# Second attention: ranks ahead of values, divisions on ACT, and two reciprocal roots on DVE

## The chip, the cores and the metric

The kernel runs on one core of a Trainium2 chip. The metric is the device time of one execution in microseconds. TensorE is called PE here, VectorE DVE, ScalarE ACT, GpSimd POOL and SyncE SP.

## The reference

A network of six residual stages over x of 2048 rows (4 batches of 512) and 128 features: a routed feed-forward, a landmark attention, the feed-forward again, a feed-forward with 32 experts (top 4) and a shared part, a windowed attention, and the experts once more. The change lies in the last two, cut to this:

```python
x = x + _L1_attn_ref(_layernorm(x), ...)      # B, S = 4, 512
    q, k, v = x @ Wq + bq, x @ Wk + bk, x @ Wv + bv
    scores = einsum('bwqd,bwkd->bwqk', qw, kw) / sqrt(8)   # 7 windows of 128 at steps of 64
    out_w = einsum('bwqk,bwkd->bwqd', softmax(scores), vw) # summed over windows, / counts
    return out @ Wo + bo
x = x + 0.5 * _L1_ffn_ref(_layernorm(x), ...)
    topk_scores, topk_idx = top_k(softmax(flat @ router_w.T + router_bias), 4)
    # 32 experts: silu(gate) * up, down; sum of the 4 chosen ones by normalised score
    out = out + silu(flat @ sgate_w.T) * (flat @ sup_w.T) @ sdown_w.T    # shared part
```

## The kernel before

The program is written engine by engine: each engine runs its instructions in the order written, and waits on counting semaphores. Rows are handled in four groups of 512, which are also the batches of this attention.

`attn1` is the second attention. For batch b, PE projects q, k and v (`project_q`, L2446, and so on), computes seven score windows (`scores`, L2469) into two banks, the even windows (half 0) in one and the odd (half 1) in the other. DVE takes the maxima (`maximum`, L2351), ACT the exponentials with their sums (`exp`, L2288), DVE the reciprocals and the products (`scale`, L2358 and L2359), PE the transposes of the weights (`turned`, L2476), ACT copies them (`evict`, L2296), PE multiplies by the values (`values`, L2485), ACT averages (`averages`, L2304), PE projects out (`output`, L2499), and DVE adds to x (`residual`, L2364).

The routing of the last stage is woven in one batch behind. For group g = b - 1: statistics on DVE ("variance", L200 to L205), the power -0.5 on POOL (`power`, L211), the normalisation on DVE ("normalised", L218), transposes on PE (L227), their copy on ACT (`copy`, L232), router logits on PE (L539), and on DVE the pieces "scores" (L482), "top", "hot", "counted", "weights" and "rows". "rows" begins with L519, which needs the ranks that PE computes in `tensor_rank` (L548 to L554, waiting for the mask of "counted"), and ends with L521, which gives the row numbers. POOL then sends the group's rows to `sorted_rows` in 16 indirect DMAs (`pool_dispatch`, L469): dispatch g. POOL's powers stand at written places between these issues: those of the attention's own groups 2 and 3 too (`norm`; `srt.norm` is the routing's).

Group 3's routing runs in the eight shared-expert steps behind the attention (L416 to L418 are their gate and up matmuls, L710 the silu, L717 the product, L749 the down matmuls); the table LATE says at which step each piece stands. Step 0 to 2 also make the first table of tiles (L660 is its last part). Then the quad loop begins: 20 quads of four pairs of 64-row tiles, each with transposes of the loaded tile (L1024), their copy on DVE (L939), the expert's matmuls and four indirect DMAs on POOL for the results. Quads 0 to 3 need dispatches 0 and 1, quads 4 to 7 dispatch 2, those from 8 dispatch 3.

At the start of the attention the last two groups of the stage before are still being summed: POOL adds pairs of returned rows (`pool_pair`), DVE adds the rest (`vector_combine`), in pieces spread over batches 0 and 1, and POOL's powers for `norm` follow.

Of the kernel before, what the change touches and what calls it, by code (L numbers as in the profile page):

```python
# [10 lines left out]
I32 = mybir.dt.int32  # L11
ALU = mybir.AluOpType
ACT = mybir.ActivationFunctionType
AX = mybir.AxisListType.X
P = 128
# [17 lines left out]
def build(nc, a, out):  # L33
# [8 lines left out]
    with ExitStack() as ctx:  # L42
# [30 lines left out]
        mv = sb("mv", [P, NT, 2])  # L73
        rstd = sb("rstd", [P, NT])
# [114 lines left out]
        class Norm:  # L189
# [3 lines left out]
            def __init__(self, first, order=None):  # L193
                self.first, self.order = first, order or range(first, first + NG)

            def statistics(self, g, ready):
# [8 lines left out]
                DVE.tensor_scalar(rstd[:, 4 * g:4 * g + 4], mv[:, 4 * g:4 * g + 4, 1], 1e-5, None, ALU.add).then_inc(*var_ready.inc)  # L205
# [7 lines left out]
            def normalise(self, g):  # L213
                DVE.wait_ge(*rstd_ready(self.order[g] + 1))
# [6 lines left out]
            def transposes(self, g, meanwhile=0, b=6):  # L221
                if self.order[g]:
                    PE.wait_ge(*xT_ready(self.order[g]))
                keep_busy(meanwhile, bank[6])
                PE.wait_ge(*xn_ready(self.order[g] + 1))
# [8 lines left out]
            def transposed(self, g):  # L234
                return xT_transposed(self.order[g] + 1)

            def ready(self, g):
                return xT_ready(self.order[g] + 1)


        norms = [Norm(NG * n) for n in range(4)] + [Norm(16, (16, 17, 19, 21)), Norm(20, (18, 20, 22, 23))]
# [178 lines left out]
        class Sorted:  # L420
# [40 lines left out]
            def pool_dispatch(self, g, power_after, other_after=(), other_norm=None):  # L461

                POOL.wait_ge(*rows_ready(g + 1))
                for i in range(4 * TOPK):
                    if i == power_after and g < NG - 1:
                        self.norm.power(g + 1)
                    if i in other_after:
                        other_norm.power(2 + other_after.index(i))
# [285 lines left out]
            def tiles(self, room):  # L754
# [353 lines left out]
                for s in (mask_ready, rank_mm, rows_ready, shared_added, combined, sorted_low_ready):  # L1108
                    s.ends(NG)
                pair_added.ends(2)  # L1110
# [41 lines left out]
            def vector_combine(self, g):  # L1152
# [4 lines left out]
                yield  # L1157
                DV(DVE.tensor_tensor(xg, b[:, :, 1, :], xg, ALU.add))
                yield
                DVE.wait_ge(*self.paired[g])  # L1160
                DVE.tensor_tensor(xg, self.pair[g], xg, ALU.add).then_inc(*combined.inc)
                yield
# [29 lines left out]
        def ffn0(updated, outer, norm, srt=None, following=None):  # L1192
# [58 lines left out]
            def pool_engine():  # L1251
# [29 lines left out]
                if srt:  # L1281
                    POOL.wait_ge(*zeroed(NE))
                    for g, transfers in enumerate((6, 4, 3, 0)):
                        srt.pool_dispatch(g, transfers)
# [940 lines left out]
        def attn1(earlier, outer, norm, srt):  # L2225
# [18 lines left out]
            sc_mm, mw_ready, ew_ready, ew_scaled = (signal(n) for n in ("sc_mm", "mw_ready", "ew_ready", "ew_scaled"))  # L2244
# [21 lines left out]
            def scalar_engine():  # L2266
# [46 lines left out]
                for b in range(B):  # L2313
                    if b:
                        srt.norm.copy(b - 1)
# [316 lines left out]
```

## Time and profile before

| what | value |
|---|---|
| median of 3 runs | 977.83 us (975.63 to 982.14) |
| the profiled execution's own time | 978.78 us |
| its span, first to last instruction | 977.3 us |
| granted clock of TensorE, mean share | 0.896 |
| busy: PE, DVE, ACT, POOL | 763.2, 548.9, 400.1, 443.1 us |

The span leaves 1.5 us of the execution outside it. Busy time is a sum of instructions; what it leaves of the span is waiting, and in this kernel no engine is near full, so the table alone names no bound.

### The profile page before, as it was taken

The page shows a single profiled execution, that of the slowest core. Times are in us where ns is not written, and L with a number is a line of the kernel's source. Part 1 is how long each engine was busy: PE and PEld are TensorE (multiplying, and loading weights), DVE is VectorE, ACT ScalarE, POOL GpSimd, SP SyncE. Part 2 cuts the span into 40 slices and gives each one's busy share as a digit, 9 for nine tenths or more (in the row PEclk, how much of TensorE's full clock was granted, in tenths as well). Part 3 has the DMA queues.
Part 4 walks back from the last instruction along what each step waited for, and adds up shares of the span by engine and source line. Part 5 has one row for each costly group of instructions (what it writes and reads, how often), then busy time and mean ns, then how long its engine had stood idle before and what let it go on. Part 6 is the DMA issues. An engine that isn't in the chain of part 4 may idle for free.

```text
span 977.3 us, 19551 instructions
## 1 busy us (share of the span) xinstructions
PE 763.2 (78%) x6738; PEld 578.4 (59%) x6738; DVE 548.9 (56%) x1656; ACT 400.1 (41%) x967; POOL 443.1 (45%) x484
## 2 busy tenths in 40 slices
PE   7979989899998898867377766788788537667767
PEld 6868756699765786755254444466566424444446
DVE  6974776578655985755345233365865415333345
ACT  4647554654363554531133334326332213333421
POOL 4646602446002546445625545541666444544551
PEclk9999998999999999888688778899888859877889
DMA  9999994900543501001233222402111222232253
GB/s 230 213 220 219 221 218 92 190 4 4 114 77 129 196 1 45 27 33 50 71 78 80 73 74 69 140 28 87 36 46 44 61 54 67 66 72 75 75 170 97
DMA packets 121056, 93.99 MB, mean 96 GB/s; under 512 B 14208, under 2 KB 111872, under 8 KB 120576
## 3 DMA queue, kind: packets, MB, share of 16 engines
q1 hardware_dynamic: 104288, 70.00, 31.9%
q0 software_dynamic: 9216, 19.68, 6.0%
q10 hardware_dynamic: 7456, 3.07, 1.5%
q8 instruction: 55, 0.90, 0.4%
q14 instruction: 41, 0.34, 0.1%
HBM read 31.76 MB, written 57.41 MB: 91 GB/s over the span
## 4 chain that ended last, share of the span: by engine, by line
PE 40%; DVE 21%; another core or an unknown queue 16%; issue 9%; ACT 8%; POOL 3%; ACTq 2%; DMA 1%; DVEq 0%; POOLq 0%
PE banks L2064 5%; PE banks L1047 4%; PE banks L749 3%; PE banks L1054 2%; PE banks L1442 2%; POOL sorted_rows L469 2%; ACT routed_scratch L875 2%; DVE hT L1351 2%; PE banks L416 2%; PE banks L418 2%; PE banks L417 2%; DVE rows_x L218 2%; PE banks L1062 2%; ACTq L912 1%
## 5 line engine op out<-in xcount | busy, mean ns | idle before, releaser
L854 POOL DMA_INDIRECT expert_rows<-y,goal x160 | 155.4, 971 | 165.9 <-DVE goal L950 87.5
L469 POOL DMA_INDIRECT sorted_rows<-rows_x,row_of x128 | 127.2, 994 | 105.5 <-DVE row_of L521 69.8
L1047 PE MATMUL banks<-routed_w,t 128*64 x320 | 104.3, 484 | 43.1 <-DVE t L939 42.7
L1310 ACT ACTIVATE ys<-banks,wtab 128x128 f32<-128x128 f32 x256 | 73.1, 370 | 81.5 <-PE banks L1442 62.0
L1047 PE MATMUL banks<-routed_scratch,t 128*64 128x256 f32 x320 | 104.9, 485 | 0.3 <-issue 0.2
L956 DVE TENSOR_TENSOR h<-sg,banks 128x512 f32<-128x512 f32 x40 | 27.5, 687 | 131.5 <-ACT sg L884 103.8
L1047 PEld LDWEIGHTS banks<-routed_w,t 128*64 128x64 f32 x320 | 51.6, 173 | 81.1 <-issue 71.0
L416 PE MATMUL banks<-x_high,w_high 128*128 128x512 f32 x192 | 87.4, 455 | 0.8 <-POOL w_low L1189 0.4
L1442 PE MATMUL banks<-w,hT 128*128 128x128 f32 x512 | 71.9, 284 | 19.2 <-DVE hT L1351 18.5
L1442 PEld LDWEIGHTS banks<-w,hT 128*128 128x128 f32 x512 | 65.7, 196 | 28.6 <-issue 22.2
L418 PE MATMUL banks<-x_high,w_low 128*128 128x512 f32 x192 | 78.8, 410 | 3.1 <-issue 3.1
L417 PE MATMUL banks<-x_low,w_high 128*128 128x512 f32 x192 | 78.6, 409 | 1.1 <-issue 1.1
L1236 POOL TENSOR_TENSOR x<-ys,x 128x512 f32<-128x512 f32 x43 | 55.0, 1279 | 52.5 <-ACT ys L1310 52.2
L892 ACT COPY hT<-banks 128x512 f32<-128x512 f32 x40 | 23.4, 585 | 120.3 <-remote 58.5
L875 ACT COPY routed_scratch<-routed_w 128x384 f32 x160 | 69.8, 510 | 5.5 <-issue 5.5
L211 POOL TENSOR_TENSOR rstd<-rstd,mhalf 128x4 f32<-128x4 f32 x24 | 26.4, 1101 | 99.0 <-DVE rstd L205 98.9
L1062 PE MATMUL banks<-routed_w,hT 128*64 x320 | 50.9, 305 | 25.0 <-issue 13.0
L884 ACT ACTIVATE sg<-banks 128x512 f32<-128x512 f32 x40 | 23.8, 594 | 97.1 <-PE banks L1047 52.1
L1351 DVE TENSOR_TENSOR hT<-sg,banks 128x512 f32<-128x512 f32 x64 | 43.8, 684 | 29.4 <-ACT sg L1318 23.5
L1062 PEld LDWEIGHTS banks<-routed_w,hT 128*64 128x64 f32 x320 | 39.3, 152 | 31.1 <-issue 30.9
L1054 PE MATMUL banks<-ident,h 128*128 128x128 f32 x160 | 31.4, 328 | 32.2 <-DVE h L956 23.7
L1062 PE MATMUL banks<-routed_scratch,hT 128*64 128x128 f32 x320 | 51.3, 306 | 6.0 <-issue 6.0
(362 smaller groups left out, 1787.9 us busy)
## 6 DMA issues: line engine op xcount, KB each, us to landing
sorted_rows<-zeros SPq DMA_DIRECT2D x32, 1120.0 KB, 16.8
tile<-sorted_rows SPq DMA_DIRECT2D x252, 35.0 KB
routed_w<-in_ffn_w SPq DMA_DIRECT2D x8, 768.0 KB, 11.7
w<-in_ffn_w SPq DMA_DIRECT2D x20, 192.0 KB, 5.3
expert_rows<-y,goal POOLq DMA_INDIRECT x160
tile<-sorted_rows ACTq DMA_DIRECT2D x68, 35.0 KB
qS<-x_high SPq DMA_DIRECT2D x8, 256.0 KB, 6.0
sorted_rows<-rows_x,row_of POOLq DMA_INDIRECT x128
```

The lines of the kernel that those rows point to most:

```text
L416: PE.matmul(ps, expert.high[:, n, :], x_high[:, cols], start=True, stop=False)
L417: PE.matmul(ps, expert.high[:, n, :], x_low[:, cols], start=False, stop=False)
L418: return PE.matmul(ps, expert.low[:, n, :], x_high[:, cols], start=False, stop=True)
L469: POOL.indirect_dma_start(sorted_rows, bass.IndirectOffsetOnAxis(self.row_of[:, g, i:i + 1], 0), rows_x[:, 4 * g + i // TOPK, :], None).th ...
L854: POOL.indirect_dma_start(expert_rows, bass.IndirectOffsetOnAxis(goal[:, 4 * q + i:4 * q + i + 1], 0), y[q % 6][:, i * P:(i + 1) * P], Non ...
L875: last = SCL.copy(odd[q % 3][:, i, :], routed.w[:, bass.ds(expert[4 * q + i], 1), :].rearrange("p o c -> p (o c)"))
L1047: last = PE.matmul(pairs(q)[ROWS * h:ROWS * h + ROWS, i, :], t[q % 2][:, rows], weights(q, i, h, slice(0, 2 * P)), start=True, stop=True)
L1062: last = PE.matmul(bank[7][ROWS * h:ROWS * h + ROWS, i * P:(i + 1) * P], hT[q % 2][:, rows], weights(q, i, h, slice(2 * P, 3 * P)), start= ...
L1236: engine.tensor_tensor(xg, ys[s % 2][:, :].rearrange("p (j d) -> p j d", d=D), xg, ALU.add).then_inc(*added.inc)
L1310: last = SCL.mul(ys[s % 2][:, j * P:(j + 1) * P], bank[4 + s % 2][:, j * P:(j + 1) * P], wtab[:, t, e:e + 1])
L1351: DVE.tensor_tensor(hT[s % 2][:, :], sg[s % 2][:, :], bank[2 + s % 2][:, :], ALU.mult).then_inc(*hidden_done.inc)
L1442: last = PE.matmul(bank[4 + s % 2][:, j * P:(j + 1) * P], hT[s % 2][:, j * P:(j + 1) * P], experts[s % rows].w[:, 2, :], start=True, stop= ...
```

## The change

In the attention's batches 1 to 3, DVE makes only the reciprocals (`reciprocals`), and ACT multiplies the windows (`divide`). The order on all engines is written anew: PE computes the ranks of a group ahead of the batch's values, ACT copies the routing's transposes behind both exponentials in batches 2 and 3, the two sums of the stage before stand together ahead of batch 0's residual, and some projections and their evictions move forward. POOL makes both powers of `norm` ahead of dispatch 0, and that of routing group 1 after its fourth issue. The routing norms of groups 2 and 3 get their reciprocal root on DVE (`root`: a shift and a multiply-add on the bits, then three Newton steps), so POOL makes no power within dispatches 1 and 2. LATE moves each piece of group 3 one step later. Signals of `Norm` get an order for the transposes (`turn`) apart from that of the powers.

```diff
     class Norm:
-            def __init__(self, first, order=None):
+            def __init__(self, first, order=None, turn=None, rooted=()):
...
-                DVE.tensor_scalar(rstd[:, 4 * g:4 * g + 4], mv[:, 4 * g:4 * g + 4, 1], 1e-5, None, ALU.add).then_inc(*var_ready.inc)
+                variance = DVE.tensor_scalar(rstd[:, 4 * g:4 * g + 4], mv[:, 4 * g:4 * g + 4, 1], 1e-5, None, ALU.add)
+                if g in self.rooted:
+                    DV(variance)
+                    self.root(g)
+                else:
+                    variance.then_inc(*var_ready.inc)
+
+            def root(self, g):
+                v, y = rstd[:, 4 * g:4 * g + 4], guess[:, :]
+                DVE.tensor_scalar(half_var[:, :], v, -0.5, None, ALU.mult)
+                DV(DVE.tensor_scalar(y.bitcast(I32), v.bitcast(I32), 1, None, ALU.arith_shift_right))
+                DV(DVE.tensor_scalar(y.bitcast(I32), y.bitcast(I32), -1.0, float(0x5f3759df), ALU.mult, ALU.add))
+                for n in range(3):
+                    DV(DVE.tensor_tensor(square[:, :], y, y, ALU.mult))
+                    DV(DVE.tensor_tensor(square[:, :], square[:, :], half_var[:, :], ALU.mult))
+                    DV(DVE.scalar_tensor_tensor(out=y if n < 2 else v, in0=square[:, :], scalar=1.5, in1=y, op0=ALU.add, op1=ALU.mult))
...
             def normalise(self, g):
-                DVE.wait_ge(*rstd_ready(self.order[g] + 1))
+                if g not in self.rooted:
+                    DVE.wait_ge(*rstd_ready(self.order[g] + 1))
...
-        norms = [Norm(NG * n) for n in range(4)] + [Norm(16, (16, 17, 19, 21)), Norm(20, (18, 20, 22, 23))]
+        norms = [Norm(NG * n) for n in range(4)] + [Norm(16, (16, 17, 19, 20), (16, 17, 19, 21)), Norm(20, (18, 21, 22, 23), (18, 20, 22, 23), (2, 3))]
...
-            LATE = dict(normalised=1, transposes=2, copy=2, logits=3, split=3, scores=3, top=4, hot=4, counted=4, exp=4, rank=5,
-                        weights=5, rows=5, low=6)
+            LATE = dict(normalised=2, transposes=3, copy=3, logits=4, split=4, scores=4, top=5, hot=5, counted=5, exp=5, rank=6,
+                        weights=6, rows=6, low=7)
...
@@ pool_engine @@
                 srt.norm.power(0)
-                srt.pool_dispatch(0, 8, (3, 9), norm)
-                srt.pool_dispatch(1, 3)
-                srt.pool_dispatch(2, 1)
-                srt.pool_dispatch(3, 0)
+                POOL.wait_ge(*xn_ready(srt.norm.turn[0] + 1))
+                norm.power(2)
+                norm.power(3)
+                srt.pool_dispatch(0, {4: 1})
+                srt.pool_dispatch(1, {})
+                srt.pool_dispatch(2, {})
+                srt.pool_dispatch(3, {})
...
@@ scalar_engine @@
+                def divide(b, h):
+                    SCL.wait_ge(*sums_ready(2 * b + h - 1))
+                    for k in range(len(HALVES[h])):
+                        w = WA * h + k
+                        last = SCL.mul(Ew[h][:, k, :], Ew[h][:, k, :], sw[:, b, w:w + 1])
+                    last.then_inc(*ew_divided.inc)
...
-                for b in range(B):
-                    if b:
-                        srt.norm.copy(b - 1)
...
+                srt.norm.copy(0)
+                exp(1, 0)
+                exp(1, 1)
+                srt.scalar_exp(0)
+                divide(1, 0)
+                divide(1, 1)
...
+                for b in (2, 3):
                     exp(b, 0)
                     exp(b, 1)
+                    srt.norm.copy(b - 1)
+                    divide(b, 0)
+                    divide(b, 1)
+                    srt.scalar_exp(b - 1)
+                    if b == 2:
+                        norm.copy(3)
                     evict(b, 0)
+                    if b == 2:
+                        evict_q(3)
                     evict(b, 1)
+                    if b == 2:
+                        evict_k(3)
                     averages(b)
+                    srt.scalar_split(b - 1)
+                    if b == 2:
+                        evict_v(3)
...
@@ vector_engine @@
+                def reciprocals(b, h):
+                    total = sw[:, b, WA * h:WA * h + len(HALVES[h])]
+                    DVE.wait_ge(*ew_ready(2 * b + h + 1))
+                    DVE.reciprocal(total, total).then_inc(*sums_ready.inc)
...
+                earlier.vector_combine(2)
+                earlier.vector_combine(3)
+                residual(0)
+                routed_piece(0, "variance")
+                norm.statistics(2, earlier.combined[2])
+                routed_piece(0, "normalised")
+                maximum(1, 0)
+                maximum(1, 1)
+                norm.statistics(3, earlier.combined[3])
+                routed_piece(0, "scores")
+                reciprocals(1, 0)
+                routed_piece(0, "top")
+                reciprocals(1, 1)
+                for piece in ("hot", "counted", "weights", "rows"):
+                    routed_piece(0, piece)
+                norm.normalise(2)
+                residual(1)
+                routed_piece(1, "variance")
+                for b in (2, 3):
+                    if b == 3:
+                        maximum(3, 0)
+                        maximum(3, 1)
+                    routed_piece(b - 1, "normalised")
+                    srt.vector_low(b - 2)
+                    if b == 2:
+                        maximum(2, 0)
+                        maximum(2, 1)
+                        norm.normalise(3)
+                    reciprocals(b, 0)
+                    reciprocals(b, 1)
+                    for piece in ("scores", "top", "hot", "counted", "weights", "rows"):
+                        routed_piece(b - 1, piece)
                     residual(b)
                     routed_piece(b, "variance")
...
@@ tensor_engine @@
+                for b in range(1, B):
                     scores(b, 0)
                     scores(b, 1)
+                    srt.norm.transposes(b - 1)
+                    if b > 1:
                         keep_busy(2, bank[5 - b % 2])
+                    srt.tensor_logits(b - 1)
+                    if b == 1:
+                        keep_busy(2, bank[4])
+                    if b == 2:
+                        norm.transposes(3)
+                    turned(b, 0)
                     if b == 1:
                         srt.tensor_rank(0)
                         PE.wait_ge(*earlier.shared[3])
-                    turned(b, 0)
                     turned(b, 1)
-                    values(b, 0)
-                    values(b, 1)
+                    if b == 2:
+                        project_q(3)
                     if b > 1:
                         srt.tensor_rank(b - 1)
+                    values(b, 0)
+                    if b == 2:
+                        project_k(3)
+                    values(b, 1)
+                    output(b)
                     if b == 1:
-                        output(1)
                         norm.transposes(2, 0, 7)
                         project_q(2)
...
```

## Rows read from the trace of the kernel before

**Rows 1.** The chain of waits that ended last, its share of the span by engine.

```profile
PE 40%; DVE 21%; another core or an unknown queue 16%; issue 9%; ACT 8%; POOL 3%; ACTq 2%; DMA 1%; DVEq 0%; POOLq 0%
```

**Rows 2.** Busy time by stretch (start:end, length, each engine's busy us and instructions).

```profile
740.00:779.00 39.00, 30.55 (x164) 23.92 (x162) 24.01 (x91) 9.04 (x19) 19.75 (x20) 0.86 0.18 51
779.00:794.00 15.00, 0.00 (x1) 0.00 (x0) 1.95 (x4) 0.23 (x1) 11.34 (x13) 0.58 0.26 72
```

**Rows 3.** POOL in order of time: start, us, instruction, idle time before and its end.

```profile
688.21 1.44 POOL L469 DMA_INDIRECT sorted_rows<-rows_x,row_of  x1 [10.57 <-DVE row_of L521]
...
711.79 0.95 POOL L469 DMA_INDIRECT sorted_rows<-rows_x,row_of  x1 [0.30 <-issue]
715.98 0.95 POOL L469 DMA_INDIRECT sorted_rows<-rows_x,row_of  x1 [3.24 <-DVE row_of L521]
...
719.88 1.04 POOL L211 TENSOR_TENSOR rstd<-rstd,mhalf 128x4 f32<-128x4 f32 x1
...
736.76 0.95 POOL L469 DMA_INDIRECT sorted_rows<-rows_x,row_of  x1 [0.30 <-issue]
741.50 0.95 POOL L469 DMA_INDIRECT sorted_rows<-rows_x,row_of  x1 [3.78 <-DVE row_of L521]
...
762.98 0.95 POOL L469 DMA_INDIRECT sorted_rows<-rows_x,row_of  x1 [0.30 <-issue]
775.62 0.95 POOL L469 DMA_INDIRECT sorted_rows<-rows_x,row_of  x1 [11.69 <-DVE row_of L521]
...
794.59 0.95 POOL L469 DMA_INDIRECT sorted_rows<-rows_x,row_of  x1 [0.30 <-issue]
```

**Rows 4.** DVE in order of time, 700 to 794 us.

```profile
701.21 1.28 DVE L218 TENSOR_SCALAR rows_x<-x,mv,rstd 128x128 f32<-128x128 f32 x4 [1.86 <-POOL rstd L211]
...
714.09 0.69 DVE L519 TENSOR_TENSOR r_home<-r_home,banks 128x512 f32<-128x512 f32 x1 [2.21 <-remote]
...
720.96 1.28 DVE L218 TENSOR_SCALAR rows_x<-x,mv,rstd 128x128 f32<-128x128 f32 x4 [1.94 <-POOL rstd L211]
...
739.61 0.69 DVE L519 TENSOR_TENSOR r_home<-r_home,banks 128x512 f32<-128x512 f32 x1 [7.27 <-remote]
...
756.38 0.28 DVE L660 CAST table<-banks 1x128 int32<-1x128 f32 x1 [3.27 <-remote]
...
766.86 0.49 DVE L482 MAX8 top<-banks 128x8 f32<-128x32 f32 x4 [9.06 <-remote]
...
793.30 0.69 DVE L939 COPY t<-banks 128x512 f32<-128x512 f32 x1 [6.34 <-remote]
```

**Rows 5.** PE in order of time, 688 to 779 us.

```profile
688.88 1.73 PE L2476 MATMUL banks<-ident,Ew 128*128 128x128 f32 x7 [3.31 <-DVE Ew L2359]
...
732.18 0.75 PE L554 MATMUL banks<-r_home,ones 128*128 128x96 f32 x6
...
737.77 2.07 PE L2499 MATMUL banks<-Wo,oT 128*128 128x128 f32 x8 [3.90 <-issue]
739.50 0.77 PE L416 MATMUL banks<-x_high,w_high 128*128 128x512 f32 x1
...
755.88 0.98 PE L539 MATMUL banks<-Wr,xnT 128*128 128x32 f32 x8
...
778.40 0.60 PE L1024 MATMUL banks<-ident,tile 128*128 128x128 f32 x4
```

**Rows 6.** Prices: order of time on DVE and ACT, and DVE's groups, 663 to 740.

```profile
711.16 0.29 DVE L513 TENSOR_SCALAR red_a<-red_a 128x4 f32<-128x4 f32 x1
...
373.15 1.14 ACT L1310 ACTIVATE ys<-banks,wtab 128x128 f32<-128x128 f32 x4 [0.69 <-issue]
...
703.30 0.58 ACT L232 COPY xnT<-banks 128x512 f32<-128x512 f32 x1 [1.76 <-PE banks L227]
...
706.19 0.25 ACT L459 ACTIVATE power<-power 128x16 f32<-128x16 f32 x1
...
L2359 DVE TENSOR_TENSOR Ew<-Ew,sw 128x512 f32<-128x512 f32 (+1 forms) x8 | 5.6, 705 | 0.3
```

More of the change, by code:

```diff
@@ L1107, in tiles @@
                 tensor_engine()
-                for s in (mask_ready, rank_mm, rows_ready, shared_added, combined, sorted_low_ready):
+                for s in (mask_ready, rank_mm, rows_ready, shared_added, sorted_low_ready):
                     s.ends(NG)
+                combined.ends(NG)
                 pair_added.ends(2)
@@ new lines, in scalar_engine @@
+                exp(0, 1)
+                evict_v(0, (1,))
+                evict(0, 0)
+                evict(0, 1)
+                norm.copy(1)
+                averages(0)
+                SCL.wait_ge(*earlier.back_here[2])
+                evict_q(1)
+                evict_k(1)
+                evict_v(1)
+                srt.norm.copy(0)
[4 more added lines that the diff above has]
+                divide(1, 1)
+                evict(1, 0)
@@ L2384, in vector_engine @@
                 last_shared_add()
-                for b in range(B):
-                    if b:
-                        maximum(b, 0)
-                        maximum(b, 1)
-                        if b == 1:
-                            next(third)
-                        elif b == 2:
-                            norm.normalise(3)
-                        for piece in ("scores", "top"):
-                            routed_piece(b - 1, piece)
-                        if b > 1:
-                            scale(b, 0)
-                            scale(b, 1)
-                        for piece in ("hot", "counted", "weights", "rows"):
-                            routed_piece(b - 1, piece)
-                        if b == 1:
-                            scale(b, 0)
-                            scale(b, 1)
-                            next(third)
-                            norm.statistics(2, earlier.combined[2])
-                            for _ in fourth:
-                                pass
-                            norm.normalise(2)
+                earlier.vector_combine(2)
@@ L2408, in vector_engine @@
                     residual(b)
                     routed_piece(b, "variance")
-                    if b == 0:
-                        next(third)
-                    elif b == 1:
-                        norm.statistics(3, earlier.combined[3])
-                    if b > 1:
-                        srt.vector_low(b - 1)
-                    if b < LAST:
-                        routed_piece(b, "normalised")
-                    if b == 1:
-                        srt.vector_low(0)
+                srt.vector_low(2)
```

92 lines of the change are left out of this document (39 added, 53 removed).

## The prediction

> **What bounds the kernel now.** I first read the chain that ended last [rows 1]: PE leads with 40% of the span, DVE has 21%, and 16% is "another core or an unknown queue", which on one core can only be a wait whose end came without a releaser that the trace knows. So no engine bounds the kernel; a relay of waits does. The stretch that the change touches is the second attention with its routing (about 663 to 740 us), the eight shared-expert steps behind it (740 to 779) and the start of the quad loop. The table by stretch [rows 2] shows PE busy 30.55 of 39 us in the shared steps, and then not at all from 779 to 794.
>
> POOL's own order comes next [rows 3]. Its four dispatches of 16 indirect DMAs each begin at 688.21, 715.98, 741.50 and 775.62. An issue every 1.265 us follows from the last one (775.62 to 794.59, 15 steps), so 16 take 20.2 us. POOL waited 3.24, 3.78 and 11.69 us ahead of dispatches 1, 2 and 3, each time for the row numbers (L521).
>
> DVE's and PE's rows say why the row numbers were late [rows 4, 5]. Rank matmuls of group 2 (L554) end at 732.18 + 0.75 = 732.93, but DVE's L519, which waits for them alone, starts at 739.61: 6.7 us of "remote". The logits of group 3 (L539) end at 756.86 and their reader starts at 766.86: 10 us. The transposes of the first tile (L1024) end at 779.00 and their copy (L939) starts at 793.30: 14.3 us. At 714.09 it is 2.21 us, at 756.38 3.27. All lie in the later part of a dispatch or just behind it: 711.79, 736.76 and 762.98 are the last issues of dispatches 0, 1, 2, and the signal came 2.3, 2.9 and 3.9 us behind them [rows 3, 4]; the copy of the first tile came 1.3 us ahead of the last issue of dispatch 3. I call this a hold: PE's signal waits while POOL dispatches. I have no cause for it, only its places. What is on the path is therefore POOL's stream with the holds at its ends.
>
> **Batch 1: divisions leave DVE.** Before, DVE scaled the weights behind all of group 0's routing, and PE waited 3.31 us for it, to 688.88 [rows 5]. Now only two reciprocals stand between the routing pieces, and ACT multiplies window by window. Four ACT multiplies of 128x128 by a column took 1.14 us [rows 6], so seven take 2.0 us, on an engine that had nothing to do then. The wait of 3.3 us goes, and the rank matmuls now stand between the two halves, which gives or takes 1 us: values, output and the projections of batch 2 come 3 to 5 us earlier. The reciprocals and the two statistics pushed ahead delay group 0's row numbers, dispatch 0 with them, by 0.5 to 1 us. The two other norms' powers now precede it; they are ready by then, so they cost no path.
>
> **Dispatch 0.** It took from 688.21 to 711.79 + 1.26 = 713.05 with three powers inside: 24.8 us. With one, 16 issues and one power of about 1.5 make 21.8. From 689.1 it ends at 711, 2 us earlier, with its power after 4 issues and not after 8, thus 4 x 1.265 = 5 us earlier. DVE's wait of 1.86 us at 701.21 [rows 4] goes with that.
>
> **Batch 2.** ACT's copy of the routing's transposes now stands behind both exponentials: before, the copy began at 703.30 and the exponentials ran to 706.19 [rows 6], about 2.4 us, which the logits now wait for. Against it stand the 5 us of the power, and two DVE scalings of 0.705 us [rows 6] that no longer lie between "top" and "hot". Sum for the row numbers of group 1: 2.4 - 5 - 1.4 = -4.0, to which the held 2.2 us may be added. They were there at 715.7, and are now at 709.5 to 714.5; so dispatch 1 starts between the end of dispatch 0, 711, and 714.5 (before 715.98), the later value if a hold still meets the ranks.
>
> **Batch 3: the root on DVE.** The power of group 2 sat in POOL's queue behind three issues of dispatch 1 (719.88), and DVE stood 1.94 us ahead of 720.96 [rows 3, 4]. Instead DVE runs 12 small dependent instructions. Their like (L513, 128x4) took 0.29 us at most [rows 6], and 0.2 with the shorter ones around it; I take 12 x 0.21 = 2.5 us, between 2.0 and 3.5. The trace shows no shift of bits; I price it as the other small ones. The Trainium skill, VectorE: DVE Perf Modes, section on the TRN2 errata, gives some 150 cycles of fixed cost to an instruction; by that the root would be an estimated 12 x 0.156 = 1.9 us, 0.6 less than my sum. Two maxima now also precede the normalisation, about 1.2 us by L2359's 0.705 for the same widths, while a subtraction of some 0.6 moves behind it. So seen from the residual this piece gains nothing (2.5 + 1.2 against 1.94 + 0.6, about +1); scalings off DVE give 1.4 back, the rest of batch 3 is what batches 1 and 2 hand on.
>
> **Ranks ahead of values.** The ranks of groups 1 and 2 no longer queue behind 14 value matmuls, some 2 us by the 0.60 that four transposes of that width took [rows 5]. Group 2's would end near 732.9 - 4 - 2 = 727, ahead of where their hold was. Then dispatch 2 waits only for dispatch 1: 711 to 714.5 + 20.2, so 731 to 735, middle 733, against 741.50: -8.5. The end of the attention (first shared matmul, 739.50 [rows 5]) held, at 737.77, a wait of 3.9 us behind held signals. I leave a hold of that size in, since values still lie late in dispatch 1, and take 732 to 736.
>
> **The combined sums, LATE and the end.** Two residual sums and their statistics move to a DVE that idled there: nothing, unless back rows are late. LATE puts every piece of group 3 one step later; a step is about 2.3 us ((756.86 - 739.50 - 3.27) / 6). Group 3's power leaves POOL (1.3 us of dispatch 2) and costs 2.5 us on DVE, under the first step. Dispatch 2 from 733 has its last issue 19 us later, 752; as before the hold ends 3.9 us behind, 755.9. The logits of group 3, now at step 4, are made near 734 + 13 + 2.3 = 749, inside it. From release to dispatch 3 were 8.8 us (766.86 to 775.62 [rows 3, 4]); so dispatch 3 starts at 764.7, or 767 if the later step shows in full: -9 to -11. If dispatch 2 starts at 735 it is -7. The first tile's copy came 17.7 us behind that start, and the loop behind it is unchanged; it hands the shift on. I take -9.5.
>
> Profiled time before 978.78, so 969.3 after; the median was 0.95 lower, so about **968.5**.
>
> **Rivals.**
> (1) Holds fade. If they sit where ranks and values happened to meet a dispatch's tail, work 5 us earlier slips ahead of them. Without them, shared steps start at 730 and take 25 us to row numbers plus one step: dispatch 3 at 757, -18: 960. The 25 are 775.4 - 739.5 less the holds of 10.0 and 3.3, and 2.3 for the step. For: the rows show no hold in the first 20 us of dispatch 0. Against: every dispatch had one. Chance 0.22.
> (2) Slower: dispatches 0 to 2 now run without POOL's pauses of 3.24 and 3.78 us. In the last hold signals took 14.3 us to come with no end of a dispatch behind them. If only a pause lets PE's signals through, a hold from 708 lasts to the end of dispatch 1 at 731 + 2.5, and batch 3 (its 20 us from there) ends at 753, 13 us later than now; group 2's row numbers come some 14 us after 733.5, at 747.5 against 741.2, and with part of the later step dispatch 3 comes 8 us later: 986. It decides once group 1's row numbers are there before dispatch 0 ends. Chance 0.18.
> (3) Nothing: the copy behind the exponentials (2.4) and the later step (2.3) eat what the batches give, and holds end where they ended, since loop start hangs on dispatch 3 alone: 975 to 979. Chance 0.14.
> (4) The division or root does not do as told, for example an ACT multiply that costs twice 0.29 us: seven then take 4 us, still beside waits; 972. Chance 0.04.
> My forecast, -7 to -11, keeps 0.42.
>
> **How the numbers follow.** A measurement of this kernel tells about 1% (9.8 us) from no change. Forecast 967 to 972 lies astride 968.05, the line of 1%: 0.45 of it counts as faster. Faster 0.22 + 0.19 = 0.41; slower is over half of rival 2, 0.10; the rest, 0.49, is within 1%. The range runs from 956, rival 1 with its batches a little better, to 984, most of rival 2 left out at its far end.
>
> **What would show it.** POOL: dispatches 0, 1 and 2 with gaps under 1 us, or with 3 us if the ranks are held; dispatch 2 near 733, dispatch 3 near 765. PE: no wait of 3 us ahead of batch 1's transposes; first shared matmul by 736. DVE: twelve small instructions of 0.17 to 0.3 us behind the statistics of groups 2 and 3, no POOL wait ahead of L218. "Remote" waits at the tails of the dispatches as before; if they are much longer within 711 to 733, rival 2; if gone, rival 1. The prediction is wrong if the loop's first tile does not follow dispatch 3's start by some 18 us, or if the holds follow something other than POOL's stream.

## The result and the profile after

The change is slower. Its median was 985.92 us (978.57 to 994.24, 20 runs) beside 977.66 us of the kernel before (965.88 to 986.62, 20 runs): 8.3 us or 0.85% more. The ratio is 1.0145, 95% interval 1.0112 to 1.0179, or 14 us; it leaves out the executions that ran in a slower state of the chip and the medians do not, so all differences of a few us here are uncertain by as much. The profiled execution took 981.63 us, its span is 980.1 us, the mean granted clock 0.889. In its records the kernel after reaches the second attention's first scores at 660.10 us, the kernel before at 663.56; from there on 3.46 us must be added to a time of after to set it beside a row of before.

The chain of waits by engine, beside [rows 1]:

```profile
PE 36%; DVE 22%; another core or an unknown queue 17%; issue 10%; ACT 8%; ACTq 3%; POOL 2%; DMA 1%; SPq 0%; DVEq 0%; POOLq 0%
```

The holds have not faded: the share with no known releaser is 17% where it was 16%. POOL in order of time, beside [rows 3]:

```profile
684.46 1.03 POOL L487 DMA_INDIRECT sorted_rows<-rows_x,row_of  x1 [5.87 <-DVE row_of L539]
...
704.68 0.96 POOL L487 DMA_INDIRECT sorted_rows<-rows_x,row_of  x1 [0.31 <-issue]
709.64 0.96 POOL L487 DMA_INDIRECT sorted_rows<-rows_x,row_of  x1 [3.99 <-DVE row_of L539]
...
728.93 0.96 POOL L487 DMA_INDIRECT sorted_rows<-rows_x,row_of  x1 [0.30 <-issue]
739.60 0.96 POOL L487 DMA_INDIRECT sorted_rows<-rows_x,row_of  x1 [9.71 <-DVE row_of L539]
...
758.56 0.96 POOL L487 DMA_INDIRECT sorted_rows<-rows_x,row_of  x1 [0.31 <-issue]
786.04 0.96 POOL L487 DMA_INDIRECT sorted_rows<-rows_x,row_of  x1 [26.52 <-DVE row_of L539]
...
813.50 0.96 POOL L872 DMA_INDIRECT expert_rows<-y,goal  x1 [7.46 <-DVE y L982]
```

Set beside [rows 3] with the 3.46 us added, dispatch 0 begins at the old time, dispatch 1 2.9 us earlier, dispatch 2 1.6 us later and dispatch 3 13.9 us later. POOL waits 9.71 and 26.52 us where it waited 3.78 and 11.69. What batches 1 and 2 gave was lost in batch 3, and much more behind it. DVE, beside [rows 4], shows on what:

```profile
707.75 0.69 DVE L537 TENSOR_TENSOR r_home<-r_home,banks 128x512 f32<-128x512 f32 x1 [4.21 <-remote]
...
711.96 0.69 DVE L2410 TENSOR_TENSOR x<-banks,x 128x512 f32<-128x512 f32 x1 [2.59 <-issue]
...
723.09 0.56 DVE L2397 TENSOR_REDUCE mw<-banks 128x3 f32<-128x384 f32 x1 [5.66 <-remote]
...
732.32 0.49 DVE L500 MAX8 top<-banks 128x8 f32<-128x32 f32 x4 [6.90 <-remote]
...
762.27 0.29 DVE L597 COPY sums<-banks 128x128 f32<-128x128 f32 x1 [11.08 <-remote]
```

The line to read first is 723.09. It takes the maxima of the second half of batch 3's scores. TensorE had finished those scores at 715.05, and the semaphore event is recorded at 723.07: held 8.0 us, in the middle of dispatch 1. Behind it in DVE's queue stands group 2's normalisation (723.57), for which PE waits 9.77 us:

```profile
724.82 1.09 PE L247 MATMUL banks<-ident,rows_x 128*128 128x128 f32 x4 [9.77 <-issue]
...
742.82 0.48 PE L436 MATMUL banks<-x_high,w_high 128*128 128x512 f32 x1
...
748.96 2.08 PE L767 MATMUL banks<-w,hT 128*128 128x128 f32 x8 [2.91 <-DVE hT L735]
...
754.43 0.63 PE L696 MATMUL banks<-ones,r_home 32*128 32x64 f32 x2
...
776.87 0.98 PE L557 MATMUL banks<-Wr,xnT 128*128 128x32 f32 x8
...
787.44 0.60 PE L1042 MATMUL banks<-ident,tile 128*128 128x128 f32 x4
```

The first shared matmul comes at 742.82, which with the 3.46 us is 6.8 us behind [rows 5]. The other 7.1 of dispatch 3's 13.9 us are lost in the shared steps. PE waits 2.91 us for the first product hT, which stands behind group 3's root in DVE's queue, and its matmuls then follow each other at 0.43 us instead of 0.23. The sums that PE has made at 754.43 + 0.63 = 755.06 reach DVE at 762.27: held 7.2 us, to 2.7 us behind the last issue of dispatch 2. Before, PE did not wait for that hT and the sums were not held; PE and DVE of before:

```profile
744.68 1.16 PE L749 MATMUL banks<-w,hT 128*128 128x128 f32 x8
748.08 0.29 DVE L579 COPY sums<-banks 128x128 f32<-128x128 f32 x1 [0.39 <-PE banks L678]
```

The stretches that answer to [rows 2]:

```profile
742.00:786.00 44.00, 32.52 (x160) 26.57 (x159) 22.70 (x93) 10.88 (x21) 13.43 (x14) 0.77 0.15 41
786.00:805.00 19.00, 5.44 (x40) 3.69 (x38) 6.48 (x20) 0.75 (x2) 14.46 (x15) 0.77 0.27 74
```

The granted clock there is 0.77, where it was 0.86: more waits, and a slower engine behind each of them. One thing went better: the first tile's transposes are not held (787.44 here, then the loop's first matmul at 790.10). The holds only moved on: the next three signals, of that tile's matmuls, the second tile's transposes and those of h, came 6.4, 10.1 and 8.2 us late. The loop's first result rows leave at 813.50 against 805.46. Without the 3.46 us, that is 8.0 us later, where dispatch 3 was 10.4 later. The rest of the loop takes back more, and the two profiled spans end only 2.8 us apart: the traces show where time was lost, but these two executions do not show the whole difference of the medians.

### The profile page after: what moved, and what is told of

Its sections match the earlier page's. It is cut to its first block, busy times and chain, and to the rows that moved or that the text cites. A ratio compares the mean times of both kernels' runs of the same rounds, so it can differ in the third digit from the quotient of the medians.

```text
span 980.1 us, 19589 instructions
## 1 busy us (share of the span) xinstructions
PE 765.1 (78%) x6738; PEld 579.2 (59%) x6738; DVE 547.8 (56%) x1674; ACT 406.5 (41%) x988; POOL 439.0 (45%) x482
## 4 chain that ended last, share of the span: by engine, by line
PE 36%; DVE 22%; another core or an unknown queue 17%; issue 10%; ACT 8%; ACTq 3%; POOL 2%; DMA 1%; SPq 0%; DVEq 0%; POOLq 0%
PE banks L2080 5%; PE banks L1065 3%; PE banks L1458 3%; ACT routed_scratch L893 3%; PE banks L767 2%; DVE hT L1367 2%; PE banks L436 2%; PE banks L438 2%; PE banks L1080 2%; PE banks L437 2%; PE banks L1072 1%; DVE rows_x L238 1%; ACTq L930 1%; POOL sorted_rows L487 1%
## 5 line engine op out<-in xcount | busy, mean ns | idle before, releaser
L1065 PE MATMUL banks<-routed_w,t 128*64 x320 | 101.7, 474 | 27.2 <-DVE t L957 24.9
L1065 PE MATMUL banks<-routed_scratch,t 128*64 128x256 f32 x320 | 101.8, 474 | 0.0
L230 POOL TENSOR_TENSOR rstd<-rstd,mhalf 128x4 f32<-128x4 f32 x22 | 22.7, 1032 | 98.0 <-DVE rstd L208 95.2
```

The lines of the kernel that those rows point to most:

```text
L1065: last = PE.matmul(pairs(q)[ROWS * h:ROWS * h + ROWS, i, :], t[q % 2][:, rows], weights(q, i, h, slice(0, 2 * P)), start=True, stop=True)
```

## The experiments

The experiments ran on four chips; whether the result came from one of them is not recorded. Beside the result and beside E1 to E4 the kernel before took 978 us; on the other three chips (E5 to E8, E9 to E12, E13 to E16) it took 806, 803 and 802 us, and there no signal of TensorE in the second attention is held for more than 0.7 us. The whole traces say the same. I set each recorded semaphore update of PE beside the end of PE's last instruction on that semaphore. In the six traces of the first kind 99 to 111 of some 750 come over 1 us late, in the twelve of the second none of some 770 (the last microsecond, where the program ends, left out). In the trace of before, 103 of the 108 late ones belong to work that ended while POOL was issuing indirect DMAs, and none of the 408 updates ahead of its first issue is late. No trace of the kernel before was kept on the last three chips. Each ratio below is against the kernel before on the same chip. The three chips without holds were not chosen, but they split the question in two: what the change costs through holds, and what without.

### E1 to E4, a chip where signals are held (before 978.62 us)

E1 puts only the two roots on DVE, into the kernel before.

```
-Norm(20, (18, 20, 22, 23))
+Norm(20, (18, 20, 22, 23), (18, 20, 22, 23), (2, 3))      # and root() as in the change
```

> The kernel before with one part of the change: the two routing norms' roots (groups 2 and 3) on DVE, and so no power within dispatches 1 and 2; all orders as before. Theory S (dispatches 0 to 2 now stream without breaks, and PE's signals are held while they stream): the powers were breaks, so holds in dispatches 1 and 2 start earlier and this alone is slower than before, by 2 to 6 us. Theory O (the new order of ACT's and PE's work is what costs): no slower than before, or up to 4 us faster, since DVE no longer waits 1.94 us for POOL and group 2's power not for three issues.

Measured 983.31 us, ratio 1.0047 (1.0003 to 1.0091): 4.7 us slower, as theory S had it. The roots alone cost, in the old order as well. But E15 below finds the same loss where nothing is held, so this run is no evidence for the breaks.

E2 is the change with the two powers back in POOL's queue.

```
-Norm(20, (18, 21, 22, 23), (18, 20, 22, 23), (2, 3))
+Norm(20, (18, 21, 22, 23), (18, 20, 22, 23))
-srt.pool_dispatch(1, {})
-srt.pool_dispatch(2, {})
+srt.pool_dispatch(1, {3: 2})
+srt.pool_dispatch(2, {1: 3})
```

> The changed kernel with the two powers back on POOL, group 2's ahead of issue 3 of dispatch 1 and group 3's ahead of issue 1 of dispatch 2. Theory S: each power is a break, so the signals of batch 3's scores are held less than the 8 us of the changed kernel, and it comes 3 to 8 us under it (ratio to before 1.005 to 1.01). Theory O: within 2 us of the changed kernel or slower by the wait for POOL (ratio 1.013 to 1.018).

Measured 972.81 us, ratio 0.9952 (0.9916 to 0.9988). The whole of the 1.0145 is gone, more than theory S expected, and the rest of the change is a small gain. Its POOL and DVE rows, in order of time:

```profile
709.75 0.95 POOL L487 DMA_INDIRECT sorted_rows<-rows_x,row_of  x1 [4.01 <-DVE row_of L539]
...
715.54 1.04 POOL L230 TENSOR_TENSOR rstd<-rstd,mhalf 128x4 f32<-128x4 f32 x1 [2.32 <-DVE rstd L208]
...
734.01 0.95 POOL L487 DMA_INDIRECT sorted_rows<-rows_x,row_of  x1 [0.30 <-issue]
...
739.35 1.41 POOL L230 TENSOR_TENSOR rstd<-rstd,mhalf 128x4 f32<-128x4 f32 x1 [4.39 <-DVE rstd L208]
...
774.46 0.95 POOL L487 DMA_INDIRECT sorted_rows<-rows_x,row_of  x1 [14.70 <-DVE row_of L539]
```

```profile
716.00 1.23 DVE L2397 TENSOR_REDUCE mw<-banks 128x4 f32<-128x512 f32 x2 [0.54 <-PE banks L2519]
...
721.39 0.49 DVE L500 MAX8 top<-banks 128x8 f32<-128x32 f32 x4 [1.91 <-PE banks L557]
```

Dispatch 1 starts at the same time as in the change (709.75, 709.64). Then POOL stands 2.32 us for the variance and computes for 1.04, and just there the scores' signals come through: both maxima run at 716.00, where the change's second one ran at 723.09. The router's maximum is at 721.39 and not 732.32, and the first shared matmul at 733.36 and not 742.82. Dispatch 2 gains little by it: its first issue, at 734.01 straight behind dispatch 1, comes 5.6 us earlier, but then POOL stands for group 3's variance and its power, and the second comes at 740.97, where the change has it at 740.87. Dispatch 3 comes 11.6 us earlier, 9.5 of which were there at the first shared matmul. So the first break, of 3.4 us, came at the right place; E2 also takes the roots out of DVE's queue, and does not tell the two apart. Nor does it end all holds: the signal for the residual at 737.05 was held 3.4 us.

E3 is the change with the old LATE.

```
-LATE = dict(normalised=2, transposes=3, copy=3, logits=4, ..., low=7)
+LATE = dict(normalised=1, transposes=2, copy=2, logits=3, ..., low=6)
```

> The changed kernel with group 3's pieces at their old steps. If the later steps cost a step, 2.3 us, it comes that much under the changed kernel (ratio about 1.012). If the pieces stand behind a held signal either way, nothing (1.0145). If an early normalisation makes PE wait behind DVE's root, 1 to 2 us slower (1.016).

Measured 990.85 us, ratio 1.0100 (1.0053 to 1.0146), with the same hold: the signal of batch 3's scores, done at 720.21, came at 731.65. What the later step costs cannot be told from it: by the ratios E3 is 4 us better than the change, by the medians (990.85 and 985.92) 5 us worse, and the intervals overlap. The hold does not need the later step.

E4 is the change with breaks: an otherwise useless power of 128x4 on POOL ahead of every fourth issue of the last stage's four dispatches.

```
+if i % 4 == 2 and pauses:
+    PO(POOL.tensor_tensor(pause[:, :], ones[:, 0:4], mhalf[:, 0:4], ALU.pow))
```

> The changed kernel with a small POOL power of constants, waited for, ahead of issues 2, 6, 10 and 14 of each of the last stage's dispatches: some 1.3 us each, 5 us a dispatch. Theory S: PE's signals come through in the breaks, so no hold over 3 us within dispatches 0 to 2, and the time falls by 3 to 10 us although POOL's stream is longer. Theory O, or a hold that no short break ends: the dispatches end 5 us later each, and the time rises by 0 to 8 us.

Measured 955.46 us (941.24 to 958.51, 6 runs), ratio 0.9768 (0.9716 to 0.9821). With sixteen useless instructions more it is the fastest kernel on this chip, 30 us below the change's median (that one beside a kernel before of 977.66), where theory S expected 3 to 10. E4 differs from the change in nothing but the breaks. The profiled execution is its fastest, 14 us below its median, and was 8.7 us ahead of the change's before any break, at its first issue of dispatch 0 (675.78 and 684.46); from there to dispatch 3 it takes 78.6 us, the change 101.6. POOL and DVE in order of time:

```profile
685.41 1.13 POOL L489 TENSOR_TENSOR pause<-ones,mhalf 128x4 f32<-128x4 f32 x1
686.83 1.03 POOL L490 DMA_INDIRECT sorted_rows<-rows_x,row_of  x1 [0.29 <-POOL pause L489]
...
754.41 0.96 POOL L490 DMA_INDIRECT sorted_rows<-rows_x,row_of  x1 [2.71 <-DVE row_of L542]
```

```profile
709.89 0.49 DVE L503 MAX8 top<-banks 128x8 f32<-128x32 f32 x4 [3.38 <-PE banks L560]
...
729.03 0.29 DVE L600 COPY sums<-banks 128x128 f32<-128x128 f32 x1 [3.12 <-PE banks L699]
...
742.98 0.49 DVE L503 MAX8 top<-banks 128x8 f32<-128x32 f32 x4 [1.48 <-PE banks L560]
...
752.52 0.69 DVE L540 TENSOR_TENSOR r_home<-r_home,banks 128x512 f32<-128x512 f32 x1 [3.07 <-remote]
```

In dispatches 0 and 1 no signal is held over 0.6 us. The first one over 2 us comes at 747.85, and the ranks that DVE reads at 752.52, at the end of dispatch 2, were held 4.4 us, against an expectation of no hold over 3 us. Dispatch 3 starts at 754.41. So the long holds go with POOL's unbroken streams of issues, and a break of a little over 1 us each four issues (some 5 us) ends most of them.

### E5 to E8, a chip without holds (before 806.35 us)

E5 is the kernel before with E4's breaks; E6 is E4 with a memset of 128x4 in place of the power; E7 is E4 with the two powers back on POOL as in E2; E8 is E4 with breaks in the first stage's dispatches too, and ahead of the third of each tile's four result DMAs.

```
-PO(POOL.tensor_tensor(pause[:, :], ones[:, 0:4], mhalf[:, 0:4], ALU.pow))
+PO(POOL.memset(pause[:, :], 0.0))                                          # E6
+if i == 2:                                                                 # E8, ahead of the result DMAs
+    PO(POOL.tensor_tensor(pause[:, :], ones[:, 0:4], mhalf[:, 0:4], ALU.pow))
```

> The kernel before with the same breaks in its last stage's dispatches (ahead of issues 2, 6, 10, 14), its own powers kept. It tells what the new order is worth once the holds are cured. Theory S with a sound new order: it gains too (holds of 2.2, 6.7, 10 and 14 us go), to a ratio of 0.980 to 0.990, and stays 2 to 8 us above the changed kernel with breaks (0.977). If the new order is worth nothing: the same 0.977. If breaks help only where the stream is tight: no gain, 0.995 to 1.005.

> As the changed kernel with breaks, but each break is a memset of 4 columns, waited for, and not a power. It tells whether it is the length of the break or that there is one. If a break of any length lets PE's signals through: ratio 0.970 to 0.978. If the length counts: between that and the changed kernel, 0.985 to 1.01, with holds of over 4 us back in dispatches 0 to 2.

> The changed kernel with breaks and also the two powers back on POOL. It tells what the root on DVE is worth by itself, with the holds gone. By the prediction's count the root gives group 2 about nothing at the residual and saves a wait of 1.9 us and up to three issues in POOL's queue: this comes 1 to 4 us above the kernel with breaks alone (ratio 0.978 to 0.981). If more breaks still help, it is under it (0.970 to 0.975).

> The changed kernel with breaks in both stages' dispatches and one break in the middle of every quad's four result DMAs. Theory S says that the 'remote' waits of the quad loops are the same holds: each of some 40 quads has one of 2 to 5 us. If a break of 1.3 us lets signals through there too, 10 to 40 us come off (ratio 0.94 to 0.965). If the loops' waits are something else, POOL's extra 1.3 us a quad is hidden in its idle time: 0.972 to 0.980, the first stage's dispatches giving 2 to 5 us.

Measured: E5 822.64 us, 1.0216 (1.0175 to 1.0257); E6 817.4 us, 1.0126 (1.0085 to 1.0168); E7 824.0 us, 1.0217 (1.0178 to 1.0257); E8 876.67 us, 1.0878 (1.0838 to 1.0919). None did what the first chip had led me to expect. What cures a hold is, where there is none, POOL time and nothing else; E8's chain of waits has 15% in the result DMAs and 4% in their breaks. I had run these four on the belief that holds belong to the kernel. They do not belong to it alone: the kernel before with breaks (E5), and with the roots (E15), shows none.

### E9 to E12, another chip without holds (before 802.81 us)

The change itself, E2, E4 and E5 once more, unaltered.

> The changed kernel once more, beside the kernel before on the same chip. The second set of runs was made on a chip where the kernel before took 806 us and its traces show no signal of PE held over 0.7 us; the first on one where it took 978 us. If this chip is one without holds: theory S says that the change is then worth what its orders are worth, by the sum without holds 0 to 8 us faster (ratio 0.990 to 1.000). If it is one with holds: 1.010 to 1.018, as measured first.

> The changed kernel with the two powers on POOL. With holds: 0.995 again. Without holds, breaks are worth nothing, and the root on DVE is worth 0 to 4 us: this is 0 to 4 us above the changed kernel.

> The changed kernel with a break of 1.3 us ahead of each fourth issue. With holds: 0.977 again. Without holds: the dispatches get 5 us longer each and stand on the path; 5 to 20 us above the changed kernel, ratio 1.01 to 1.02.

> The kernel before with the breaks. With holds, not yet measured there: 0.980 to 0.990 if the new order is worth a little by itself, 0.977 if it is worth nothing. Without holds: 1.02 again.

Measured: the change 809.67 us, 1.0100 (1.0075 to 1.0124); with powers back 805.03 us, 1.0010 (0.9985 to 1.0035); with breaks 816.5 us, 1.0164 (1.0125 to 1.0204); before with breaks 819.71 us, 1.0198 (1.0161 to 1.0235). E11 and E12 came as expected. E9 and E10 did not: the change was to be 0 to 8 us faster than before, and E10 0 to 4 us above it. So the change is slower without any hold as well, and again it is the roots: E10 differs in nothing else. Here the records can be followed step by step. DVE in E9:

```profile
620.68 0.17 DVE L208 TENSOR_SCALAR rstd<-mv 128x4 f32<-128x4 f32 x1
620.88 0.17 DVE L218 TENSOR_SCALAR half_var<-rstd 128x4 f32<-128x4 f32 x1
...
622.93 0.16 DVE L224 SCALAR_TENSOR_TENSOR rstd<-square,guess 128x4 f32<-128x4 f32 x1
623.13 1.15 DVE L2397 TENSOR_REDUCE mw<-banks 128x4 f32<-128x512 f32 x2
...
638.02 0.69 DVE L2410 TENSOR_TENSOR x<-banks,x 128x512 f32<-128x512 f32 x1 [1.52 <-PE banks L2549]
...
642.69 0.69 DVE L547 TENSOR_TENSOR x_low<-xnT,x_high 128x512 fp32r<-128x512 f32 x1
643.30 0.68 DVE L735 TENSOR_TENSOR hT<-sg,banks 128x512 f32<-128x512 f32 x1
```

and in E10:

```profile
620.83 0.23 DVE L208 TENSOR_SCALAR rstd<-mv 128x4 f32<-128x4 f32 x1
621.24 1.23 DVE L2397 TENSOR_REDUCE mw<-banks 128x4 f32<-128x512 f32 x2 [0.17 <-PE banks L2519]
622.92 1.28 DVE L238 TENSOR_SCALAR rows_x<-x,mv,rstd 128x128 f32<-128x128 f32 x4 [0.46 <-POOL rstd L230]
...
635.61 0.69 DVE L2410 TENSOR_TENSOR x<-banks,x 128x512 f32<-128x512 f32 x1 [1.51 <-PE banks L2549]
...
637.74 0.68 DVE L547 TENSOR_TENSOR x_low<-xnT,x_high 128x512 fp32r<-128x512 f32 x1
638.34 0.68 DVE L735 TENSOR_TENSOR hT<-sg,banks 128x512 f32<-128x512 f32 x1
```

Group 2's root runs from 620.88 to 623.09 in E9. In E10 the maxima start 0.4 us behind L208 and POOL makes the power beside them; DVE waits 0.46 us for it. E9 is 1.9 us later at the maxima and 2.4 us later at the residual sum (638.02, 635.61). Group 3's root then takes 2.5 us more, ahead of x_low and of the first product hT of the shared steps: from the residual sum to hT it is 5.28 us in E9 and 2.73 in E10. PE waits for that hT:

```profile
644.03 1.16 PE L767 MATMUL banks<-w,hT 128*128 128x128 f32 x8 [3.10 <-DVE hT L735]
...
645.69 0.63 PE L438 MATMUL banks<-x_high,w_low 128*128 128x512 f32 x1
646.11 0.63 PE L436 MATMUL banks<-x_high,w_high 128*128 128x512 f32 x1
...
652.59 0.39 PE L438 MATMUL banks<-x_high,w_low 128*128 128x512 f32 x1
```

In E10 that wait is 0.50 us. Behind the longer one E9's matmuls follow each other at 0.43 us and not 0.23 for some 7 us, that is at 1.2 GHz in place of 2.4. The windows from the first shared matmul to dispatch 3, of E9:

```profile
637.70:670.80 33.10, 27.85 (x155) 22.74 (x153) 23.07 (x93) 10.17 (x20) 16.23 (x18) 0.90 0.20 57
```

and of E10:

```profile
635.30:664.00 28.70, 24.74 (x155) 20.23 (x153) 20.85 (x81) 10.02 (x20) 19.72 (x22) 1.00 0.26 71
```

with a granted clock of 0.90 and 1.00. So of the 6.8 us by which dispatch 3 is later (670.77 against 664.00), 2.4 stand behind group 2's root, 2.5 behind group 3's, and 1.9 are left for the clock. The spans differ by 6.0, the medians by 4.6 us.

### E13 to E16, a third chip without holds (before 801.93 us)

E13 is the change with group 3's root made right ahead of its normalisation, two shared steps later. E14 adds group 2's power on POOL, inside dispatch 1. E15 is E1 again, E16 is E13 with E4's breaks.

```
 if g in self.rooted:
     DV(variance)
-    self.root(g)
+    if g < NG - 1:
+        self.root(g)
...
+elif g == NG - 1:            # in normalise
+    self.root(g)
```

> The change with one thing moved: group 3's root (12 instructions, 2.5 us) is made by VectorE right ahead of group 3's normalisation in the shared steps, where its result is first read, and no longer behind the statistics, ahead of the subtraction for x_low and the first products of the shared steps. Work and values are the same. Theory A (the root stands in VectorE's queue ahead of work that TensorE waits for; in the traces of e9 and e10 dispatch 3 starts at 670.8 and 664.0, of which 2.4 at group 2's root, 2.5 at group 3's and 1.8 at the lower clock that follows the longer wait): 4 us faster than the change, so where signals are not held (before near 805) ratio 1.005, where they are held (before near 978) about 1.010. Theory B (only POOL's stream without pauses counts): as the change, 1.010 or 1.0145. Theory C (the later place costs the same again, since the normalisation is awaited there): as the change.

> As e13, and group 2's root goes back to a power on POOL, inside dispatch 1 ahead of its issue 3. Theory A: both terms of the root are off the path, so as with both powers back: 1.000 without holds (805), and 0.995 to 1.000 with holds. Theory B: where signals are held the break in dispatch 1 is worth about as much as in e2 and that in dispatch 2 is missing, about 1.00 to 1.005; without holds 1.010 as the change.

> The kernel before with the two roots alone, as in e1, beside the runs above. Theory A: where signals are not held the roots cost the kernel before 2 x 2.5 us and part of the lower clock, 4 to 7 us: 1.005 to 1.009; where they are held 1.0047 as measured in e1. Theory B: without holds 1.000, since POOL's powers were no more than breaks.

> As e13, with the four breaks of 1.1 us in each of the last stage's dispatches of e4. Theory A: 4 us faster than e4 or e11: 0.973 where signals are held, 1.011 where they are not. Theory B: 0.977 and 1.0164.

Measured: E13 802.44 us, 1.0032 (0.9990 to 1.0073); E14 801.87 us, 1.0017 (0.9972 to 1.0063); E15 806.31 us, 1.0063 (1.0023 to 1.0102); E16 816.25 us, 1.0203 (1.0155 to 1.0251). E13, E14 and E15 came where theory A had them; E13 changes nothing but a place in DVE's queue and takes back some two thirds of what the change costs here (1.0032 against 1.0100, on another chip without holds). E14 takes group 2's root off DVE as well and should by theory A be some 4 us faster than E13; it is 0.6 us faster by the medians, so group 2's share is read from the traces of E9 and E10 and no run confirms it. E13's wait for the first hT:

```profile
641.33 1.16 PE L770 MATMUL banks<-w,hT 128*128 128x128 f32 x8 [0.67 <-DVE hT L738]
...
649.85 1.97 PE L770 MATMUL banks<-w,hT 128*128 128x128 f32 x8 [0.83 <-DVE hT L738]
```

From the first shared matmul (637.43) to dispatch 3 (667.89) it takes 30.5 us, between 33.1 and 28.7; what is missing to E10's is once more the clock, which falls at another place: 0.94 is granted in this stretch, and the half pace begins at 649.85, behind a wait of 0.83 us. E10 has the same wait at the same step and keeps its clock. So the longer wait of E9 comes ahead of a fall, but the length of one wait does not decide it, and that it caused the fall is not shown. E15 says that the roots cost the old order as much: 4.4 us here, 4.7 in E1.

E16 missed. Theory A gave 1.011. With breaks, dispatches 0 to 2 are one stream: 48 issues of 1.265 us and 12 breaks of about 1.3 make 76 us. In E11 it runs from 599.45 to 675.2, and dispatch 3 begins 1.88 us behind it; in E16 from 604.47, and the first issue of dispatch 3 (681.11) follows the last of dispatch 2 (679.85) at once. Without holds the breaks make POOL the bound, so an earlier row number buys next to nothing there (in E11 at most those 1.88 us).

## Why the prediction was wrong

It said 968.5 us, -9.3; it was +8.3.

**The step that failed** is "Batch 3: the root on DVE", in its conclusion that "seen from the residual this piece gains nothing" with the power's place in POOL's queue counted as a mere 1.94 us wait. The price of the root was right: 12 instructions took 2.2 us in E9 (I had 2.5; the estimate from the Trainium skill's fixed cost, VectorE: DVE Perf Modes, section on the TRN2 errata, was 1.9, and the trace lies between the two: each instruction is busy for 0.16 us, but most start 0.2 us apart). Two things were not.

**POOL's power was a break.** In both powers I saw only work. In E2, the power and POOL's wait for it let the scores' signal through at 716.0; in the change that signal is held 8.0 us, in E3 11.4, and in E4, which keeps the roots and adds breaks, at most 0.6. This is my rival 2, with its mechanism ("if only a pause lets PE's signals through") and near its time (986 against 985.92), but not with its condition: dispatches 0 and 1 did not merge, since group 1's row numbers were held too, and POOL stood 3.99 us at 709.64. The hold began behind that pause, 5.4 us into dispatch 1. That its time fits is in part luck: it had dispatch 3 8 us later, which came 13.9 us later, and the loop took the rest back. I gave it 0.18 because every hold in the trace before seemed to sit at a tail [rows 4]; the 14.3 us hold in mid-stream was in front of me, and I used it as the ground of this rival only. The sum also let the holds stay where and as long as they had been ("as before the hold ends 3.9 us behind"); the runs showed 8.0 us in mid-dispatch 1 and 7.2 us in dispatch 2 on sums that had not been held. (Rival 1 has a slip: 730 plus its 25 us is 755 and not 757, for the 25 hold the later step already; it would have read some 957 us.)

**The roots stand ahead of awaited work.** I counted group 2's root once and put group 3's "under the first step", at nothing. The cover was not there: x_low and hT queue behind it, and PE waits for hT. Without holds this gives 2.4 + 2.5 us and a lower clock behind the longer wait, and it is most of E9's 1.0100. The change's own trace has the second part too, the wait of 2.91 us at 748.96.

**LATE** I had priced at up to 2.3 us; E3 neither confirms nor refutes it. **Dispatch 1** was forecast for 711 to 714.5 and came at 713.1 on the clock of before, **dispatch 0** at 687.9 for 689.1: batches 1 and 2 were right. **Dispatch 2** (731 to 735) came at 743.1, and **dispatch 3** (764.7 to 767) at 789.5, both behind the hold, with the roots' share in it. The loop's first tile was to be copied 17.7 us behind dispatch 3's start; it was copied 3.3 us behind it, not held. Three later signals were held in its place, so that the first results got back only 2.4 us. A first tile that does not follow by some 18 us was one of my own signs of a wrong prediction.

**What the rest of the change is worth**: with powers on POOL, 0.9952 where signals are held and 1.0010 where not. The 3 to 5 us that I gave batch 1 are about all of it (4.7 us by E2's ratio), and without holds there is nothing.

How much of the 1.0145 is the hold and how much the roots' place was not separated on a chip with holds: E13 landed on a chip without. E1 and E15 agree on 4.5 us for the roots in the old order, with holds and without; so as far as these two can tell (each to some 4 us) the powers were worth nothing as breaks there, and it took the new order for a break in dispatch 1 to matter. The difference between the change and E2, 1.9 points or 13.1 us by the medians, mixes both, and may be taken across two chips. If the roots' place costs there what E9 and E10 show (0.9 points, 4.6 us), an estimate of 8 to 12 us is left for the breaks. The kernel before with breaks was never measured where signals are held, so how much of E4's 0.9768 the old order would have got too is open.

## What to carry to other kernels

A small instruction moved to another engine costs its own time only if nothing that is awaited stands behind it in the new queue, so read the queue behind the insertion and not the engine's idle share; a root that is needed two steps later belongs two steps later. Before work is taken out of a queue of DMA issues, look whether signals elsewhere come through just where that work stood. Measure on more than one chip: breaks were worth 2.3% on one and cost 1.3 to 2.2% on three others.

## What the hardware showed that I had not expected

The same kernel took 978 us in two sets of runs (one chip or two) and 802 to 806 us on three other chips. In the first, semaphore updates of TensorE came up to 14 us late in this stretch while POOL issued indirect DMAs, on the three others less than 0.7 us late under the same stream; the cause is open. Where it happens, a break of 1.0 to 1.3 us ahead of every fourth issue took the long holds from three dispatches, all but a few of 2.2 to 4.4 us at the end of the third (E4). A matmul stream that followed a wait of 3.1 us ran at half its pace for some 7 us (E9), and did not where the wait was 0.5 us (E10); in E13 it did behind a wait of 0.83 us.
